# Cross-attention bands in a fused attention and expert kernel: where the copies of the attention outputs stand, one more place for them, and an earlier down-projection tile

## The reference

```python
x = x + xattn_ffn(layernorm(x), ctx)     # x: 4 x 2048 tokens x 512, ctx: 4 x 77 x 384
x = x + moe(layernorm(x))                # 8 experts, hidden 128, top-1 gate

def xattn_ffn(x, y):
    q = x @ Wq + bq;  k = y @ Wk + bk;  v = y @ Wv + bv      # 16 heads of 32
    attn = softmax(q k^T / sqrt(32))                          # over the 77 text tokens
    out = attn v
    return relu(out @ W1 + b1) @ W2 + b2                      # 512 -> 1024 -> 512
```

## Time and profile before

| what | value |
|---|---|
| median of three runs | 1566.11 us |
| the profiled execution | 1562.44 us, of which the span of its instructions is 1560.4 us |
| TensorE busy | 1445.3 us, 93% of the span |
| VectorE busy | 1013.9 us, 65% |
| ScalarE busy | 613.4 us, 39% |
| GpSimd busy | 330.3 us, 21% |
| mean granted TensorE clock | 0.971 of full speed |
| longest chain, by engine | TensorE 72%, VectorE 16%, ScalarE 6% |

### The profile page before, as it was taken

One profiled execution on the slowest core, in us unless ns is written; L12 is line 12 of the kernel. 1 busy time (PEld: TensorE's weight loads), 2 busy tenths in 40 slices (PEclk: granted clock), 3 DMA queues, 4 the chain that ended last, 5 costly groups with the idle time before them and its releaser, 6 DMA issues.

```text
span 1560.4 us, 23319 instructions
## 1 busy us (share of the span) xinstructions
PE 1445.3 (93%) x8254; PEld 1064.9 (68%) x8254; DVE 1013.9 (65%) x2155; ACT 613.4 (39%) x1145; POOL 330.3 (21%) x292
## 2 busy tenths in 40 slices
PE   7898999899998989999999989899989989899998
PEld 5375757666675757676675757576766757578897
DVE  5566666576767666685767566666756565747666
ACT  4343333342323333242424233332424242328886
POOL 1140201102020202011020202020110202005886
PEclk9799999999999989999999989999999999999999
DMA  6200201102120202021021203020110203156985
GB/s 263 67 28 1 81 1 49 47 28 79 35 68 28 88 28 88 28 65 55 21 74 38 73 28 102 5 82 0 42 41 1 82 1 108 55 196 204 319 264 165
DMA packets 56914, 118.12 MB, mean 76 GB/s; under 512 B 8329, under 2 KB 16786, under 8 KB 55906
## 3 DMA queue, kind: packets, MB, share of 16 engines
q1 hardware_dynamic: 46002, 82.93, 17.1%
q0 software_dynamic: 10800, 33.70, 5.6%
HBM read 73.77 MB, written 44.66 MB: 76 GB/s over the span
## 4 chain that ended last, share of the span: by engine, by line
PE 72%; DVE 16%; ACT 6%; issue 3%; DMA 1%; SPq 1%; POOL 0%; ACTq 0%; POOLq 0%; DVEq 0%
PE bank L1123 23%; PE bank L1148 16%; PE bank L964 11%; DVE att L1063 10%; ACT E L1042 6%; PE bank L1048 5%; PE bank L1548 3%; PE bank L1586 2%; PE bank L1201 2%; DVE att L1076 2%; PE bank L1223 2%; PE bank L989 2%; DVE mx L1002 2%; PE bank L1034 2%; PE bank L1532 1%
## 5 line engine op out<-in xcount | busy, mean ns | idle before, releaser
L1148 PE MATMUL bank<-w,actH 128*128 128x512 f32 x1536 | 389.3, 405 | 0.0
L1123 PE MATMUL bank<-actA,w 128*128 128x512 f32 x1536 | 375.8, 398 | 1.3 <-DVE actA L1094 1.3
L1148 PEld LDWEIGHTS bank<-w,actH 128*128 128x128 f32 x1536 | 291.4, 195 | 81.9 <-issue 23.2
L1123 PEld LDWEIGHTS bank<-actA,w 128*128 128x128 f32 x1536 | 285.1, 189 | 64.5 <-issue 4.0
L1063 DVE RECIPROCAL att<-bank 128x512 f32<-128x512 f32 x64 | 214.7, 3355 | 115.4 <-PE bank L1048 115.4
L964 PE MATMUL bank<-actA,wq 128*128 128x512 f32 x768 | 184.2, 392 | 25.0 <-DVE actA L944 25.0
L1089 POOL TENSOR_TENSOR actA<-att,actA 128x512 fp32r<-128x512 f32 x48 | 61.2, 1275 | 616.6 <-ACT actA L1083 616.6
L964 PEld LDWEIGHTS bank<-actA,wq 128*128 128x128 f32 x768 | 141.5, 188 | 55.5 <-issue 28.6
L1002 DVE TENSOR_REDUCE mx<-bank 128x4 f32<-128x308 f32 x256 | 104.8, 473 | 105.5 <-PE bank L989 105.5
L1083 ACT ACTIVATE actA<-att 128x512 fp32r<-128x512 f32 x64 | 40.4, 632 | 313.0 <-DVE att L1076 313.0
L1298 POOL DMA_INDIRECT region<-rows,pos x64 | 63.6, 993 | 451.5 <-DVE pos L1292 413.3
(11 more groups left out here) (175 smaller groups left out, 1818.7 us busy)
## 6 DMA issues: line engine op xcount, KB each, us to landing
rowB<-region SPq DMA_DIRECT2D x71, 258.0 KB, 3.8
xn<-in_x SPq DMA_DIRECT2D x64, 256.0 KB, 3.0
rows<-in_x SPq DMA_DIRECT2D x64, 256.0 KB, 3.3
w_raw<-in_W SPq DMA_DIRECT2D x2, 2048.0 KB, 12.2
e_raw<-in_E SPq DMA_DIRECT2D x16, 256.0 KB, 3.2
region<-padrow SPq DMA_DIRECT2D x9, 258.0 KB, 2.4
e_parts<-e_high SPq DMA_DIRECT2D x8, 256.0 KB, 2.0
e_parts<-e_low SPq DMA_DIRECT2D x8, 256.0 KB, 2.2
```

The source lines that it names most:

```text
L1123: mm = pe.matmul(p[:], w, a, start=k == 0 and j == 0, stop=k == KD - 1 and j == 2)
L1148: mm = pe.matmul(p[:], a, w, start=m == 0 and j == 0, stop=m == MF - 1 and j == 2)
```

## The change

- `OUT` is taken out of `outputs`. It now stands behind the exponentials of the group ahead: `OUT` of group 0 behind the exponentials of group 1, and so on. For group 1 the first exponential stands ahead of `MT` 1 and the other three behind it.
- The outputs are written to `att` and `csb` in turn (`att_of`); `csb` is otherwise used for the gate's logits, which fall in another part of the block. `RC` of group g waits for GpSimd's `OUT` of group g - 2 in place of g - 1.
- `Y` of subtile 1 is moved from behind the queries of block b+1 to ahead of them.
- `E2_HIGH`, `E2_LOW` and `E2_STORE` are moved up among the queries.
- In the first block the order is changed likewise: the rounded copies of `W1` (`CONV_W1`) stand among its queries, the scores of group 1 ahead of the outputs of group 0, `VP` 1 to 3 behind the exponentials, and the last outputs behind `HK` 1. The value projections of the other three contexts are staged in `xn[1]` to `xn[3]`, not in tiles of their own; the loads of the second block's `xn` wait until these are stored, and the load of `Eb1` into `csb` waits for the first block's outputs.

```diff
@@ outputs
             step("AV", b, g)
             step("NORM", b, g)
-            step("OUT", b, g)
@@ first block
         step("XLOAD", 0)
+        step("CONV_W1", 0)
         step("Q", 0, 1)
         maxima(0, 0)
         step("QLO", 0, 1)
-        step("CONV_W1", 0)
+        step("CONV_W1", 1)
         step("Q", 0, 2)
         maxima(0, 1)
         step("QLO", 0, 2)
+        step("CONV_W1", 2)
...
         exponentials(0, 0)
+        maxima(0, 3)
+        step("CONV_W1", 3)
+        scores(0, 1)
+        outputs(0, 0)
+        exponentials(0, 1)
+        step("MT", 0, 1)
+        step("OUT", 0, 0)
         step("VP", 1)
-        maxima(0, 3)
         step("VF", 1)
         step("VSTORE", 1)
-        outputs(0, 0)
-        scores(0, 1)
-        exponentials(0, 1)
-        step("MT", 0, 1)
+        outputs(0, 1)
+        scores(0, 2)
+        exponentials(0, 2)
+        step("OUT", 0, 1)
         step("VP", 2)
...
         outputs(0, 2)
         scores(0, 3)
         exponentials(0, 3)
+        step("OUT", 0, 2)
+        step("VP", 3)
@@ block loop
             step("HK", b, 1)
-            if b == 0:
+            if not b:
                 outputs(b, g)
+                step("OUT", b, g)
+                step("VF", 3)
+                step("VSTORE", 3)
             step("HK", b, 2)
...
-                if b == 0 and m < 2:
-                    step("CONV_W1", m + 2)
...
+                step("Y", b, 1)
                 step("Q", b + 1, 0)
                 step("QLO", b + 1, 0)
                 step("Q", b + 1, 1)
                 maxima(b + 1, 0)
                 step("QLO", b + 1, 1)
+                if prep is not None:
+                    step("E2_HIGH", prep)
                 step("Q", b + 1, 2)
                 maxima(b + 1, 1)
                 step("QLO", b + 1, 2)
+                if prep is not None:
+                    step("E2_LOW", prep)
+                    step("E2_STORE", prep)
                 step("Q", b + 1, 3)
                 step("MT", b + 1, 0)
                 maxima(b + 1, 2)
                 step("QLO", b + 1, 3)
-                step("Y", b, 1)
                 scores(b + 1, 0)
                 exponentials(b + 1, 0)
-                if prep is not None:
-                    step("E2_HIGH", prep)
                 step("YA", b, 2)
                 maxima(b + 1, 3)
                 outputs(b + 1, 0)
                 scores(b + 1, 1)
-                exponentials(b + 1, 1)
+                step("EXP", b + 1, 1, 0)
                 step("MT", b + 1, 1)
-                if prep is not None:
-                    step("E2_LOW", prep)
-                    step("E2_STORE", prep)
+                for h in range(1, HG):
+                    step("EXP", b + 1, 1, h)
+                step("OUT", b + 1, 0)
                 step("Y", b, 2)
                 outputs(b + 1, 1)
                 scores(b + 1, 2)
                 exponentials(b + 1, 2)
+                step("OUT", b + 1, 1)
                 step("YA", b, 3)
                 outputs(b + 1, 2)
                 scores(b + 1, 3)
                 exponentials(b + 1, 3)
+                step("OUT", b + 1, 2)
                 step("Y", b, 3)
@@ sp_xnload
+                if b == 1:
+                    sp.wait_ge(st_v, 16 * (NB - 1))
@@ sp_vstore
-            sp.dma_start(v_parts[i - 1], v_f[i - 1][0:M]).then_inc(st_v, 16)
+            sp.dma_start(v_parts[i - 1], xn[i][0:M]).then_inc(st_v, 16)
@@ sp_eb1load
+            sp.wait_ge(S["dve_o"], 1)
+            sp.wait_ge(S["pool_o"], KD - 1)
@@ dve_rc
+        def att_of(g):
+            return (att, csb)[g % 2]
...
-            if g:
-                dve.wait_ge(S["pool_o"], (KD - 1) * b + g)
-            dve.reciprocal(att[:], of("SUMS", b, g)[:]).then_inc(S["dve_rc"], 1)
+            if g >= 2:
+                dve.wait_ge(S["pool_o"], (KD - 1) * b + g - 1)
+            if b and g == 0:
+                dve.wait_ge(S["pool_o"], (KD - 1) * b)
+            dve.reciprocal(att_of(g)[:], of("SUMS", b, g)[:]).then_inc(S["dve_rc"], 1)
@@ act_h
                 act.wait_ge(S["dve_k"], KD)
-                act.wait_ge(st_v, 16 * (NB - 1))
```

## The result

The changed kernel took 1439.6 us (median of four runs, 1438.1 to 1440.96) against 1566.4 for the kernel before: a ratio of 0.919, 95% interval 0.9175 to 0.9207. Forecast were 1447 us and a range of 1434 to 1485. The profiled execution took 1438.1 us, with a span of 1436.2. The four runs lie apart by the clock: two had a mean of 0.997 and took 1438.1 and 1438.45 us, two had 0.995 and 0.996 and took 1440.75 and 1440.96; only the first was profiled.

What follows compares the result with a forecast made beforehand. A chain of waits through VectorE and ScalarE, between transposes and last sums, held up TensorE (93% busy). 15 x 7.5 + 6.4 = 118.9 off 1562.4 gives 1443.5; the median stands 3.7 above: 1447 us, range 1434 to 1485.

Steps and rivals of the forecast that it cites:

- rival 1: VectorE becomes the bound in the bands; TensorE waits some 2 us a block: 1477 us; chance 0.13.
- rival 2: The clock swings on in the bands, 1.7 us a block, now on the path: 1473 us; chance 0.10.
- rival 3: The sums wait for something else at the same place; only the queries' 1.1 us is left: 1549 us; chance 0.05.
- rival 4: Slower: a TensorE without rest is granted less clock, near 0.90 over a period; at 0.88, 1587 us; chance 0.04.
- Bands, 6.44 a block: Scores of group 0 to last sums of a block: 22.52 us in place of 28.96, with `OUT` behind the next exponentials.
- `Y` 1, 1.1 a block: Ahead of the queries, `Y` 1 fills their 1.66 us wait; a new 0.53 us wait comes at the scores; gain 1.1.
- The first block, 6.4: First scores to last up-projection chunk: 30.6 us in place of 37.0, a gain of 6.4, bounds 3 and 9.
- Two places: Reciprocals' waits for GpSimd's `OUT` two groups back are met 4 us ahead; GpSimd beside a reciprocal: 0 taken, bound 0.9.
- `E2` steps, nothing: `E2_HIGH` and `E2_LOW`, one operation each on ScalarE and VectorE between query products where both rest: no cost.
- So I count no gain from the clock: Over a block's period: no gain counted, though 5.1 us of clock are lost at 0.94 against 1.7 at 0.98.
- the period is no longer: a slower TensorE only eats its own waits: The period at clock 0.94 was read as 85.50 us against 85.55 at 0.98, the chain setting the time.
- The rule of depth-cycling: Frequent tiny TensorE idles make its clock swing; by it the clock of before would not be won back; 0.53 wait counted free.

Runs made afterwards that it cites:

- the first experiment: The kernel before with only `OUT` of a group moved behind the exponentials of the group ahead, in the first block likewise: 1465.5 us, ratio 0.934.

## Why the prediction was right, and which step of it failed

The path of it held: the exponentials were held up only by `OUT`, TensorE became the bound, and the mechanism is shown by the first experiment alone. No rival came: VectorE gates nothing in the periods (rival 1), their clock no longer swings (rival 2), the sums no longer wait (rival 3), and TensorE almost without rest runs at 1.00 in all periods but the first, which has 0.98 (rival 4). The terms, in the profiles' own time:

- **Bands, 6.44 a block.** Measured 28.96 - 22.77 = 6.19. The covers were right in size: 0.6 us at the exponentials of group 1 (forecast 0.4), 0.63 at L1113 (forecast 0.5), the second measured by using it up. Scores, sums and matmuls together took 0.25 more than laid out.
- **`Y` 1, 1.1 a block.** Measured 1.45. The new wait came as forecast, 0.46 for 0.53. What was left out is that a wait also costs the overlap of successive matmuls. The prediction let `Y` 1 start where the transposes end; in the kernel after it starts 0.25 us before that (the rows are below). An estimate from these numbers is 1.66 + 0.25 - 0.46 = 1.45. That this error and the one of the bands, 0.35 too little and 0.25 too much, nearly cancel is luck.
- **The first block, 6.4.** Measured 37.02 - 30.65 = 6.37. The wait for L1113 is 3.35 (6.9 - 3.3 = 3.6 laid out), and the clock behind it was 0.50 over 68 to 70 us.
- **Two places.** 0.22 us a block of those 6.19; GpSimd beside a reciprocal costs nothing (363.03 beside 363.71: 3.36 us, as the earlier trace rows).
- **`E2` steps, nothing.** Confirmed in the periods.

The last transposes, `Y` 1 and the queries in the kernel after:

```profile
328.48 1.04 PE L945 MATMUL bank<-ident,xn 128*128 128x128 f32 x8
329.27 2.98 PE L1166 MATMUL bank<-w,actH 128*128 128x512 f32 x12
332.09 5.60 PE L977 MATMUL bank<-actA,wq 128*128 128x512 f32 x24
```

The step that failed is "So I count no gain from the clock", and with it "the period is no longer: a slower TensorE only eats its own waits". It rests on a window that wasn't a period. (Nor does the window of 446 to 448 us in the earlier trace rows hold the queries' wait, as the prediction says, but its last 0.45 us; over the whole wait, 444.79 to 446.45, the clock was 1.00 too.) Of the kernel before, two periods at 0.94 took 88.14 and 88.09 us where their like took 85.55, and a third took 85.99 where 85.05 is usual: 2.6 + 2.5 + 0.9 = 6.0 us that a steady clock gives back. The windows of the longer period show how (columns as above):

```profile
562.00:564.00 2.00, 2.00 (x16) 0.60 (x12) 2.00 (x1) 0.00 (x0) 0.00 (x0) 0.53 0.73 257
564.00:566.00 2.00, 2.00 (x14) 1.07 (x7) 1.90 (x2) 0.00 (x0) 0.00 (x0) 0.50 0.02 5
...
578.00:580.00 2.00, 2.00 (x16) 0.38 (x15) 0.97 (x1) 0.00 (x0) 0.00 (x0) 0.79 0.03 8
580.00:582.00 2.00, 2.00 (x12) 1.71 (x9) 2.00 (x1) 0.56 (x1) 0.00 (x0) 0.50 0.00 0
```

And the timeline of TensorE across them:

```profile
560.81 1.07 PE L1048 MATMUL bank<-E,one 77*32 77x512 f32 x8 [1.82 <-ACT E L1042]
...
565.09 4.80 PE L1148 MATMUL bank<-w,actH 128*128 128x512 f32 x12
569.82 1.06 PE L1048 MATMUL bank<-E,one 77*32 77x512 f32 x8
...
577.91 1.07 PE L1048 MATMUL bank<-E,one 77*32 77x512 f32 x8 [2.13 <-ACT E L1042]
...
586.89 0.60 PE L1201 MATMUL bank<-ident,rows 128*128 128x128 f32 x4
```

The clock falls to its lower level (0.50, 1.2 GHz) a little after the waits of 1.82 and 2.13 us. Behind the first, twelve matmuls take 4.80 us instead of 3.0; the next sums, which would have waited, come without a wait and 9.01 us after the last ones, against the 8.08 of a group's chain: 0.93 lost. Behind the second lies the up-projection, in which nothing waits: 8.98 us to `TT` 3 instead of 7.36, 1.62 lost. Together 2.55, the period's excess. A slower clock is free only as far as a wait is left in front of it. In the usual period there is one fall (0.50 over 478 to 480 us); it shows as the second of the three waits being 0.63 and not some 2 us, and is free:

```profile
478.00:480.00 2.00, 2.00 (x18) 1.00 (x11) 1.90 (x2) 0.00 (x0) 0.00 (x0) 0.50 0.25 96
```

That part of the step was right.

The account: 118.9 forecast, + 6.0 for the clock, + 0.2 x 15 for the passages (7.5 forecast, about 7.7 measured without the clock), - 0.3 because the first scores start later (36.32 for 36.06), - 3.5 because the expert phase was longer by these two profiles (157.3 before, 160.8 after). That makes 124.1; measured are 1562.4 - 1438.1 = 124.3. By the medians the gain missed the forecast by some 2 us more, since the median stands 1.5 us above the profiled execution where 3.7 was taken over from before.

Where the 3.5 come from stays open, but they need not be the edit's. In the nine profiles of the experiments the length of the phase goes with the chip and launch: 161.0 to 162.4 us in the first four, which share a chip, 156.0 to 158.2 in the next four on another, 161.5 in the last on a third. Kernels close to that of before are in both groups (`OUT` moved alone in the first, `Y` 1 ahead alone and the order of before in the second), and so are kernels close to that of after. The longer ones have waits of a few us at its matmuls (in the kernel after, L1566). Whether the chip, the launch or something else sets it wasn't told apart, nor is it on record on which chips the profiles of before and after were taken.

The rule of depth-cycling that the prediction weighed (the Trainium skill, "TensorE: Matmul & The Clock Gate", section "A second HAM failure mode: psum-queue depth-cycling") speaks of frequent tiny idles. No run here is a fair test of it: 15 waits of 0.46 us, one a period, left the clock of the periods at 1.00, while the waits of about 2 us went with 0.98 down to 0.94 in the periods of the kernel before and 0.92 in the run with `Y` 1 ahead alone.

## What to carry to other kernels

When one engine's queue holds an operation that the next group needs behind one that only a later stage needs, swap them first, and lay out the bound engine's work from the starts of its instructions; here that forecast the bands to 0.25 us a block. Set windows on the true ends of a period before saying that a lower clock costs nothing, and ask what lies behind each fall: a wait absorbs it, a full stretch does not. A step that removes one wait can be worth little while other waits remain, and much once they are gone, as `Y` 1 was here, so single edits don't add up. And before a difference in a stretch that no edit touches is put down to an edit, look whether it goes with the chip and launch.

## What was not expected of the hardware

One and the same wait of 1.63 to 1.65 us, in the first block, was followed by a clock of 1.00 in the kernel after and three others, and by one of 0.66 and 0.83 in three more (over 38 to 48 us), at a cost of 1.6 to 3.2 us up to the scores of group 2 (counted from those of group 0); nothing in these traces tells which it will be. And removing the queries' waits of 1.66 us alone lowered the mean clock of the whole run from 0.971 to 0.956, though TensorE then rested less.
